# A decoder kernel on one core: a new table of places in the order of its first phase

## What is computed

```python
x = x + _L0_attn_ref(_layernorm(x), W_in, conv_w, conv_b, W_xproj, D, W_out)   # gated convolution
x = x + _L0_xattn_ref(ctx_1024, _layernorm(x), ctx_1024, Wk, Wq, Wv)           # 16 heads of 16
x = x + _L0_ffn_ref(_layernorm(x), gate_w, gate_b, w1, b1, w2, b2)             # 32 experts, 2 chosen, capacity 154
x = x + _L1_attn_ref(_layernorm(x), Wq, Wk, Wv, Wo, bo)                        # causal, adaptive temperature
x = x + _L1_xattn_ref(_layernorm(x), ctx_1024, ctx_1024, fside, ...)
x = x + _L1_ffn_ref(_layernorm(x), ln1_w, ln2_w, wqkv, wo, gate_w, w13, w2)    # attention block and 8 experts
```

## Time and profile before

| | |
|---|---|
| median of 3 runs | 1497.61 us (1496.89 to 1501.08) |
| the profiled execution: time / span | 1500.05 us / 1498.2 us |
| TensorE busy | 1311.3 us (88%) |
| VectorE, ScalarE, GpSimd busy | 783.7, 686.7, 536.2 us |
| mean granted clock of TensorE | 0.952 |
| phase A / phases B and C | 0 to 383.8 us / 383.8 to 1498.2 us |

### The profile page before, as it was taken

The page is one execution under the profiler, slowest core; times in us unless marked ns, Lnnn a source line. Parts: engine busy times, 40 slices in busy tenths (PEclk is TensorE's granted clock), DMA queues, the critical chain, the costliest instruction groups (busy, mean ns, idle before and its releaser), DMA issues. The chain is left out here.

```text
span 1498.2 us, 22969 instructions
## 1 busy us (share of the span) xinstructions
PE 1311.3 (88%) x8390; PEld 985.8 (66%) x8390; DVE 783.7 (52%) x1791; ACT 686.7 (46%) x1254; POOL 536.2 (36%) x777
## 2 busy tenths in 40 slices
PE   3999898988899999896667998899889869999996
PEld 2767575766799999895335665656556645666664
DVE  2586877775111111112556687977867555443332
ACT  1565564743222233221346777768767536221221
POOL 1103140311100000002787888777868022322222
PEclk9999999998999999998678999999989979999998
DMA  9628090930777877742100011010010444322221
GB/s 347 242 74 224 6 274 5 245 93 9 244 268 261 263 267 267 288 156 80 42 1 4 1 47 33 1 47 15 5 47 16 191 140 127 58 41 43 41 41 12
DMA packets 70686, 171.00 MB, mean 114 GB/s; under 512 B 8508, under 2 KB 47425, under 8 KB 60464
## 3 DMA queue, kind: packets, MB, share of 16 engines
q1 hardware_dynamic: 54944, 144.39, 29.8%
q0 software_dynamic: 10224, 16.09, 5.1%
q10 hardware_dynamic: 5408, 9.04, 1.6%
HBM read 123.11 MB, written 48.07 MB: 114 GB/s over the span
## 5 line engine op out<-in xcount | busy, mean ns | idle before, releaser
L1174 ACT ACTIVATE b_ht<-ps,b_b 128x154 f32<-128x154 f32 x256 | 85.0, 386 | 203.3 <-PE ps L1141 185.4
L1189 DVE TENSOR_SCALAR b_yt<-ps,b_b 128x154 f32<-128x154 f32 x64 | 21.2, 374 | 245.0 <-PE ps L1154 245.0
L2350 PE MATMUL ps<-experts,d_xt 128*128 x312 | 147.1, 594 | 1.2 <-ACT d_xt L2406 0.8
L1141 PE MATMUL ps<-b_xet,ring 128*128 128x154 f32 x1024 | 143.0, 297 | 5.4 <-ACT b_ht L1174 5.4
L1141 PEld LDWEIGHTS ps<-b_xet,ring 128*128 128x128 f32 x1024 | 137.6, 192 | 5.5 <-issue 5.5
L1154 PE MATMUL ps<-b_ht,ring 128*128 128x154 f32 x1024 | 139.7, 294 | 0.4 <-DVE b_yt L1189 0.4
L1154 PEld LDWEIGHTS ps<-b_ht,ring 128*128 128x128 f32 x1024 | 136.3, 189 | 0.6 <-issue 0.6
L2492 POOL DMA_INDIRECT out_dram<-d_yd,d_to x39 | 60.6, 1553 | 158.5 <-DVE d_yd L2464 146.6
L1623 POOL MEMSET experts<- 128x480 f32 x2 | 1.0, 507 | 316.4 <-POOLq L1084 316.4
L1503 DVE TENSOR_REDUCE c_mx<-ps 128x8 f32<-128x1024 f32 x64 | 77.8, 1216 | 65.0 <-PE ps L1450 64.6
L1466 PE MATMUL ps<-cf,experts 128*128 128x128 f32 x512 | 73.8, 292 | 23.0 <-ACT experts L1536 12.5
(11 more groups left out here) (334 smaller groups left out, 2868.4 us busy)
## 6 DMA issues: line engine op xcount, KB each, us to landing
ring<-in_w SPq DMA_DIRECT2D x64, 1024.0 KB, 5.2
xd<-zero SPq DMA_DIRECT2D x6, 3120.0 KB
a_kp<-in_ctx_k SPq DMA_DIRECT2D x8, 1024.0 KB, 16.8
experts<-in_wd SPq DMA_DIRECT2D x1, 7424.0 KB
d_xd<-xd SPq DMA_DIRECT2D x39, 130.0 KB, 2.1
xe<-zero SPq DMA_DIRECT2D x1, 4928.0 KB, 32.8
b_xe<-xe SPq DMA_DIRECT2D x32, 154.0 KB
ye<-b_ye ACTq DMA_DIRECT2D x32, 154.0 KB
```

Source lines behind the costliest of these rows:

```text
L1141: r = pe.matmul(ps[:, b, CAP * (m % 2):CAP * (m % 2) + CAP], w1r[:, slot, k, P * m:P * m + P], xet[:, e % 2, k, :], start=(k == 0), stop=( ...
L1174: r = a.activation(ht[:, e % 2, m, :], ps[:, b, CAP * (m % 2):CAP * (m % 2) + CAP], ACT.Gelu, bias=b1[:, e, m:m + 1])
L2350: m = pe.matmul(ps[:, b, :], xt[:, j % 2, k, :], w13[:, bass.ds(e, 1), f:f + F1], start=(k == 0), stop=(k == KD - 1))
```

## The change

All numbers of the table `AT_A` are new; nothing else is. No instruction, transfer, buffer or wait is added or taken away, and SyncE's queue is in the same order. Two lines of the table, and the pieces of the choice of the last block:

```diff
-    "n0s": (0, 1.1, 3.1, 4.9, 49, 62.2, 131.6, 144.9), "n0p": (1.2, 2.3, 4.3, 6.1, 50.2, 63.3, 132.8, 146.1),
+    "n0s": (0, 1.1, 24.1, 25.2, 49.6, 54.7, 133.1, 146.2), "n0p": (1.2, 2.3, 25.3, 26.4, 50.8, 55.9, 134.2, 147.4),
...
-    "gap": (None, 98.8, None, 179.5, None, 260.7, 334.9, 341.2), "weights": (None, 99.6, None, 179.9, None, 261.5, 335.5, 342.6),
+    "count": (None, 101.8, None, 180.1, None, 260.6, 336.8, 343.9), "weights": (None, 102.8, None, 181.8, None, 262.2, 337.2, 344.7),
```

More of the change, by code:

```diff
@@ L485 @@
 AT_A = {
[47 rows of a table removed]
-    "choose": (None, 95.2, None, 176.2, None, 257.1, 332.6, 338.4), "count": (None, 97.8, None, 178.9, None, 259.7, 334.9, 341.7),
-    "gap": (None, 98.8, None, 179.5, None, 260.7, 334.9, 341.2), "weights": (None, 99.6, None, 179.9, None, 261.5, 335.5, 342.6),
[14 rows of a table removed]
[47 rows of a table added]
+    "choose": (None, 98.8, None, 177.4, None, 257.8, 332.7, 340.7), "gap": (None, 101.4, None, 181.3, None, 261.7, 335, 343.1),
+    "count": (None, 101.8, None, 180.1, None, 260.6, 336.8, 343.9), "weights": (None, 102.8, None, 181.8, None, 262.2, 337.2, 344.7),
[14 rows of a table added]
 }
```

## The result

The change runs in 1477.47 us (median of 4 runs, 1475.01 to 1479.6), the kernel before beside it on the same chip in 1497.25 us (1495.92 to 1501.08): ratio 0.985, 95% interval 0.9827 to 0.9873. It is 19.8 us faster, where 17.1 were forecast. The forecast of 1480.5 is 0.9888 of the 1497.25 beside it: just outside the first interval, inside the second. (The ratio of 0.985 is not the quotient of the two medians, which is 0.987.)

What follows compares the result with a forecast made beforehand. TensorE, busy 88% of the span, was taken as the bound, so only its pauses could shrink. Start 17.6, middle 0, end -0.5 gave 17.1 us off the median 1497.6: 1480.5 us, range 1475 to 1488 (8 in 10).

Steps and rivals of the forecast that it cites:

- The start: Phase A up to `wo` of block 1: TensorE no longer waits for tokens of later blocks; 17.6 us gained.
- the cover of the tokens: Start, VectorE: tokens of block 2 land at 26.85, some 2.6 us before their statistics, so that wait is gone.
- part of the first quarter may be fast already: Start, TensorE's first projection quarter: half of it already at the higher clock would give 0.9 us more.
- The middle: From `wo` of block 1 to the end of block 6: pieces reordered, same cover in both orders; 0 us.
- the 5 us bound: Middle: a sixth of TensorE's 31.6 us idle time won or added again, 5 us either way.
- The end: From the last attention sum: later `t2` of block 6 makes `lg` wait; 0.5 us charged, bounds 0 and 1.5.
- `count` of block 6 moves behind `t2` of block 7: End, TensorE: this `count` fits into the 0.69 us in which TensorE waited for the copy.
- the 24.3 us: From the last `gate` to phase B: all orders as before, so this time stays.
- Given back in the middle: Rival, chance 0.13: units wait 0.25 us more in each of 32 attention units, 8 us; 1488.5 us.
- slower: Rival, chance 0.02: each unit's subtraction waits for one more VectorE pass, 1.23 us, 39.4 us in all; 1519.9 us.
- the wait only moves: Rival, chance 0.03: VectorE reaches block 2's statistics before their tokens and holds up `bcs` and all sums; 1485 to 1497 us.
- More is won: Rival, chance 0.07: a quarter of TensorE's 31.6 us idle time in the middle is won, 8 us; 1472.5 us.

Runs made afterwards that it cites:

- Experiment 1: The old table with only the statistics of blocks 2 and 3 and their inverse roots moved behind the convolution of blocks 0 and 1: 1482.51 us, ratio 0.9911.
- second trace: The change run again with no edit, compared with the kernel before: 1477.2 us (6 runs), ratio 0.9875 [0.9853, 0.9898].
- Experiment 8: Experiment 1 plus one wait: GpSimd's `xs` of thread 0 starts only after the choice of the round before: 1479.61 us (2 runs), ratio 0.9873.
- experiment 4a: The change with only the last `gap` on ScalarE moved ahead of the copies `ki1` and `ki2`: 1476.85 us (2 runs), ratio 0.9872.
- 9: number 7 with block 7's `av0` and its copy `vi0` moved behind the sum and the norm of block 7: 1461.08 us, ratio 0.9762.
- number 7: 4b plus one wait: GpSimd's `xs` of thread 0 starts only after the choice of the round before: 1463.12 us, ratio 0.9764.
- 4b: The change with the last `gap` and `count` ahead of the projections and copies before them, and `weights` ahead of copy `vi1`: 1469.89 us, ratio 0.9828.

## Where the forecast held, and the step that failed

**The start** was forecast at 17.6 us. It measured 18.65 in the first trace of the change and 17.60 in the second, where `wo` of block 1 stands at 49.42 and `bcp` at 25.09 (49.4 and 25.1 were forecast). Experiment 1 shows that 17.3 of it come from the two statistics alone. The chain was right link by link: no idle time of VectorE at the statistics of block 2, `bcp` at 24 to 25, then 19.4 us to `wo` of block 0 and 4.9 to that of block 1. Only the cover of the tokens was smaller, 1.8 us instead of 2.6: the statistics start at 28.13, where 29 to 31 were expected. The 1.05 us by which the two traces differ are the bound of the forecast that part of the first quarter may be fast already: a record of the projection goes from 0.63 to 0.38 us at 10.8 in one and at 12.9 in the other, and the 64 records of the quarters take 14.72 and 15.80 us. The Trainium skill, "TensorE: Matmul & The Clock Gate", Part 1, says that the number of slow matmuls varies from run to run; the two traces agree, with 1.1 us.

**The middle** is the step that failed: "I take 0: the cover is the same in both orders". Up to the last `gate` it measured 4.8 us (4.5 in the second trace), at the edge of the 5 us bound: 3.0 us to `wo` of block 7, 1.9 of them in the segment of round 1's choice, and 1.8 us behind it. The bound was wide enough; the 0 in it had no reason, since a different order is just what moves the meetings and the waits. Two things were overlooked. VectorE's busy time was taken as its work, though part of it was standing still: five meetings with `xs` stretch its instructions by 10.6 us in all before (2.0 us each in round 1's cast and in round 0's `a_ohs`), 7.3 us in the change. And TensorE's waits were counted as a sum, never asked for by what ended them. (The clock's slow stretch behind round 0's choice was overlooked as well, but both orders have it, so it is no part of the 4.8.) The waits of TensorE answer that at once. Before (60 to 360 us; total, times, longest):

```profile
PE ps L455 <- DVE a_ohs L439: 9.3, 4, 3.6
```

The change (42 to 337 us):

```profile
PE ps L455 <- DVE a_ohs L439: 3.2, 2, 1.9
PE ps L253 <- DVE a_rows L245: 2.8, 1, 2.8
```

Of 31.6 us idle time, 9.3 stood at `count`, behind the choice. In the new order 3.2 are left, and 2.8 are there at the rows of block 7, where it was 0.3 (row at 357.78 of the earlier trace rows). Experiment 8 shows in the old order what of it the meetings made: with `xs` behind the choice it has 6.0 us, and the 3.6 us wait at block 6's `count` stays, which is the old order of the end.

**The end** was charged 0.5 us for the later `t2` of block 6. It was a gain: the last stretch became 1.5 to 1.8 us shorter (48.18 to 46.42 and 46.72; it is counted in the middle's 4.8). "`count` of block 6 moves behind `t2` of block 7 and fits into the 0.69 us" had the right instruction and left out that the 3.6 us in which TensorE waited for it went with it; 2.76 us of wait at `t2` of block 7 took part of their place. Behind the last `gate` the 24.3 us became 23.45 and 23.86, with the same order; the granted clock is 0.78 there before and 0.86 in the change. The order was read rightly: `gap` alone costs and brings nothing (experiment 4a). That about 4 us lay in the same place, in `count` and `weights`, was not seen.

**The rivals.** "Given back in the middle" and "slower" are refuted by the windows, "the wait only moves" by the row at 28.13. "More is won" asked for 8 us, against 4.8 of the middle and about 1 of the clock in the better trace. The forecast had the direction, and for the start the mechanism, the place and the size. It had no mechanism for the middle and the wrong sign at the end. That the medians are only 2.7 us from it is partly luck: phase A alone became 22.5 and 24.2 us shorter in the two traces, against 17.1 forecast, and the whole time shows 19.8 and 19.6 of that.

**What stays open.** First, the 2.4 us of lead that the new order has without `xs`: they lie 0.16, 0.48, 0.62 and 1.13 us in the four stretches; for the last one the waits above are a reading, and no run took them apart. Second, phase B starts 22.5 to 24.2 us earlier in the two traces, and the medians differ by 19.8 and 19.6. In experiment 1 phase B starts 18.3 us earlier, and the interval is worth 9.6 to 17.2 us. Phases B and C spread so widely from run to run that I can't say whether they give something back.

## What to carry to other kernels

An engine that goes through its queue in order should never stand at a wait for data of a later stage while work for the next stage is behind it: two statistics moved behind the convolution were worth 17 us of the first phase, and the whole remaining table 5. Ask TensorE's idle time by what ended it before calling its sum a stock, and look in each group of small instructions for one that is ten times as long as its sisters: it stands still beside something, and here it cured as much to let GpSimd's long instruction start behind the short chain that others wait for as to leave it out. When an order holds a result back, move the instructions that consume it (`count` with `weights`, some 4 us) and not one beside them (`gap`, 0). Compare stretches at the same granted clock: the same instructions with the same waits took 1.7 us more in one trace than in another.

## What the hardware showed that was not expected

**VectorE stands still beside GpSimd.** While GpSimd runs the product of two tiles in SBUF (128x1024, 2.35 us), some of VectorE's instructions wait for its end: the cast of 8 columns took 2.18 us instead of 0.17, the tensor_scalar on 4 columns 2.09 instead of 0.16, and `a_ohs` before, from 128x128 to bf16 with 0.29 us elsewhere:

```profile
120.88 2.35 DVE L439 TENSOR_TENSOR a_ohs<-a_oh 128x128 bf16<-128x128 f32 x1
```

So do the scalar_tensor_tensor forms with both tiles in SBUF (L802, L837). Those that read one input from PSUM (L829, L831, L823) and the MAX8 and FIND_INDEX8 of the choice kept their times. GpSimd's own instruction kept its 2.34 to 2.41 us, but for the six meetings of experiments 7 to 9 in which a convolution operation of VectorE was already under way when it started: there it took 2.45 to 2.47. In number 7 VectorE's L802 starts at 180.83, and then comes:

```profile
181.06 2.46 POOL L906 TENSOR_TENSOR a_arena<-a_arena 128x1024 f32<-128x1024 f32 x1 [8.24 <-DVE a_ohs L439]
```

The time shows as busy time of VectorE and not as a wait, which is why no view of waits names it. The Trainium skill, "SBUF — State Buffer", section "Who interferes with whom", states such a lock on a port pair that the two engines share: a VectorE instruction with two SBUF inputs contends with a GpSimd instruction that reads SBUF, and so does one in a 2-port mode, which casts and tensor_scalars can enter; of the latter it says that whoever issues first has the pair for the whole instruction and the other is blocked. The traces agree in which instructions stop and in that they go on when GpSimd's ends; they do not show which mode the cast and the tensor_scalar were in.

**Phases B and C spread.** From phase B's first instruction to the end it took 1114.4 us before and 1113.6, 1106.8, 1107.6, 1105.0 in the change, its repeat and experiments 4b and 9, and 1116.7 in experiment 8, all with the same program behind phase A's end. The mean granted clock goes along: 0.952, 0.955, 0.958, 0.959, 0.959 and 0.953 of the whole span. All 13 traces fall in two groups: five at 1105.0 to 1108.5 us with 0.958 to 0.961, eight at 1110.7 to 1116.8 us with 0.952 to 0.955. An edit that is worth under 10 us has to be read in the phase where it is made, or from many runs.
